# Cross-attention and expert FFN on one core: the transpose of the probabilities taken from TensorE to VectorE and DMA

## The chip, the core and the metric

The kernel runs on one core of a Trainium2 chip. A core has TensorE (matrix products into PSUM), VectorE, ScalarE and GpSimd (elementwise work), SyncE (which here issues most DMAs) and 16 DMA engines that move data between the chip's main memory (HBM) and the on-chip SBUF, or inside SBUF. PSUM has eight banks. Each engine runs its own instructions in order; engines wait for each other through semaphores. The metric is the device time of one execution in microseconds; a run's time is the median of several executions.

## The reference, cut to what matters

All data is f32. 32 batch elements (b), each with 128 tokens and 128 context rows, width 256; 16 heads of 64.

```python
lat = layer_norm(_layernorm(x)); ctx = layer_norm(ctx_1024)
q = lat @ Wq                                     # 128 x 1024 for each b
k, v = split(concatenate([ctx, lat]) @ Wkv)      # 256 keys for each b
dots = einsum('bhid,bhjd->bhij', q, k) * 64 ** -0.5
attn = softmax(dots, axis=-1)                    # 128 x 256 for each b and head
x = x + (einsum('bhij,bhjd->bhid', attn, v) -> 128 x 1024) @ Wout
# FFN on z = _layernorm(x): each token goes to the one of 8 experts with the largest z @ centroids.T
x = x + [z + sigmoid(affinity) * (relu(layer_norm_e(z) @ w1_e.T + b1_e) @ w2_e.T + b2_e)]
```

Product attn @ v sums over keys. TensorE sums over the partition axis of both operands, while softmax leaves queries on the partitions, so the probabilities have to be transposed: 128 x 256 values for each of 16 heads and 32 batch elements.

## The kernel before, in words

**Attention.** Batch elements go in 16 pairs (g). A pair takes four steps (r = 0 to 3), each with four heads for both elements of the pair: 64 steps u = 4g + r. Most operands are split into a high and a low part and multiplied in three passes (`PASSES`), the high part being written by ScalarE and the low part by VectorE. The V product and all transposes are plain f32 products.

In step u TensorE runs, in this order: `scores(u)` (12 pairs of small products into PSUM banks 0 to 3, one bank for each n = 2 * element + parity of the head); the transposes of the last step's probabilities n = 2 and 3, with the keys of step u+1 (`keys`, L508) between and behind them; in steps with r = 0 or 1 the transposes of the next pair's normalised inputs (`normed_t`, L487); a value product (`values`, L536); `transposes(u, 0)`; the queries of step u+1 (L522); `transposes(u, 1)`; the second value product; work of the last pair's rows (`ranks`, `wout`, `z_transposes`, `affinities`: a w_out product of 24 in steps r = 0 and 1); and last `outputs(u)`, the V product (L585), for element 0 of step u and element 1 of step u-1.

Around it: VectorE takes the row maxima of a bank of scores (`maxima`, L1048), ScalarE takes the exponentials and their sums (`exponentials`, L823), VectorE inverts the sums (L1054), GpSimd multiplies (`soften`, L1408), TensorE transposes (L564), VectorE copies the result from PSUM (`copy_transposed`, L1059), TensorE multiplies by V, ScalarE and VectorE split the result (`high_outputs` L832, `low_outputs` L1092). The probabilities have a single buffer: the exponentials of step u write where those of step u-1 stood.

**What sets the order.** Everything is written out by hand, for each engine, in `for u in range(n_steps)`. The results of TensorE other than scores go through PSUM banks 4 to 7 in turn. `bank_order` lists all these items in TensorE's order; item j has bank 4 + j % 4 and may begin once item j - 4 has been read.

**FFN.** Tokens' rows are written to a table in HBM, sorted by expert, with indirect DMAs (`scatter`); blocks of 256 rows (slots, 19 here) are read back and multiplied by their expert's w1 (`layer_1`, three passes) and w2 (`layer_2`, plain f32). The first slots run between and behind the last attention steps. SyncE loads each slot's weights (1 MB for w1, 1 MB for w2), rows and vectors, and before that writes eight pieces of padding of 792 KB (`filler`) behind the sorted rows.

## Time and profile before

| | |
|---|---|
| median of 3 timed runs | 1252.53 us (1252.13 to 1253.19) |
| the profiled execution | 1252.2 us, its span 1250.4 us |
| mean granted TensorE clock | 0.993 of full speed |
| busy: TensorE, VectorE, ScalarE, GpSimd | 1202.6, 830.0, 681.9, 531.6 us |
| DMA | 77.26 MB, 62 GB/s over the span |

A busy time adds up the time in which at least one instruction of the engine was in flight. TensorE's instructions overlap one another, so the time that a group of them really takes is read from its start and the start of the next group. In a group's row "idle before" is the engine's idle time ahead of it, and the engine named behind the arrow is what ended it. Lines (L564) are those of the kernel before.

### The profile page before, as it was taken

How to read it: one execution, taken by the hardware profiler on the slowest of the kernel's cores; microseconds unless marked ns; L12 is line 12 of the kernel's file. 1: busy time of each engine (PE TensorE's matmuls, PEld its weight loads, DVE VectorE, ACT ScalarE, POOL GpSimd, SP SyncE). 2: the span in 40 equal slices, each digit the busy share in tenths (PEclk: the TensorE clock that was granted, in tenths of full speed). 3: DMA queues.
4: the chain of work that ended last, by engine and by line, in shares of the span. 5: the costliest groups of instructions: out<-in, count | busy, mean ns of one | idle time of the engine just before them, and what ended most of it. 6: DMA issues, size and time to landing. Idle time of an engine off the chain costs nothing.

```text
span 1250.4 us, 26458 instructions
## 1 busy us (share of the span) xinstructions
PE 1202.6 (96%) x9730; PEld 1071.2 (86%) x9730; DVE 830.0 (66%) x2030; ACT 681.9 (55%) x1853; POOL 531.6 (43%) x716
## 2 busy tenths in 40 slices
PE   4899999999999999999999999999998899999995
PEld 4788888888888888888888888888887799999995
DVE  5566767677777777776868676777777665444441
ACT  4565646555656565555646464555555454545541
POOL 0454545454454444444445444545433452333321
PEclk9899999999999999999999999999999999999998
DMA  5000000000000000000000000000046435656560
GB/s 186 18 9 2 23 5 23 9 24 10 18 10 18 10 19 10 18 17 11 23 6 22 6 22 6 27 2 10 1 161 198 153 122 197 234 182 237 185 214 25
DMA packets 38116, 77.26 MB, mean 62 GB/s; under 512 B 6493, under 2 KB 30045, under 8 KB 33120
## 3 DMA queue, kind: packets, MB, share of 16 engines
q1 hardware_dynamic: 33808, 65.93, 15.8%
q0 software_dynamic: 3360, 8.53, 1.8%
q8 instruction: 82, 1.34, 0.4%
q10 hardware_dynamic: 816, 1.05, 0.3%
q14 instruction: 50, 0.41, 0.1%
HBM read 60.48 MB, written 15.79 MB: 61 GB/s over the span
## 4 chain that ended last, share of the span: by engine, by line
PE 89%; DVE 4%; ACT 3%; issue 1%; POOL 1%; DMA 0%; ACTq 0%; SPq 0%; POOLq 0%; DVEq 0%
PE psum L508 13%; PE psum L536 12%; PE psum L669 11%; PE psum L585 9%; PE psum L564 9%; PE psum L654 8%; PE psum L552 8%; PE psum L522 7%; PE psum L597 7%; ACT prob L823 1%; PE psum L487 1%; PE psum L605 1%; PE psum L612 1%; DVE neg_max L1048 1%; PE psum L633 1%
## 5 line engine op out<-in xcount | busy, mean ns | idle before, releaser
L1408 POOL TENSOR_TENSOR prob<-prob,inv_sum 128x512 f32<-128x512 f32 x256 | 266.0, 1040 | 370.8 <-DVE inv_sum L1054 369.3
L823 ACT ACTIVATE prob<-psum,neg_max 128x256 f32<-128x256 f32 x512 | 237.0, 472 | 95.6 <-DVE neg_max L1048 95.6
L1059 DVE COPY prob_t<-psum 128x512 f32<-128x512 f32 x256 | 174.5, 682 | 33.2 <-PE psum L564 33.0
L1048 DVE TENSOR_REDUCE neg_max<-psum 128x2 f32<-128x512 f32 x256 | 163.7, 681 | 0.0
L564 PE MATMUL psum<-ident,prob 128*128 128x128 f32 x1024 | 156.8, 276 | 1.7 <-ACT v_n L904 1.0
L564 PEld LDWEIGHTS psum<-ident,prob 128*128 128x128 f32 x1024 | 119.5, 140 | 28.2 <-ACT v_n L904 1.5
L832 ACT ACTIVATE head_out_hi<-psum 128x512 fp32r<-128x512 f32 (+1 forms) x65 | 38.4, 590 | 184.6 <-PE psum L585 182.8
L669 PE MATMUL psum<-w,v_n 128*128 128x256 f32 x608 | 134.4, 379 | 0.0
L585 PE MATMUL psum<-prob_t,v_n 128*64 128x128 f32 x2048 | 126.1, 276 | 1.1 <-DVE prob_t L1059 1.1
L669 PEld LDWEIGHTS psum<-w,v_n 128*128 128x128 f32 x608 | 114.2, 190 | 14.7
L585 PEld LDWEIGHTS psum<-prob_t,v_n 128*64 128x64 f32 x2048 | 110.7, 137 | 9.8 <-issue 5.3
L1477 POOL DMA_INDIRECT out<-x_in,r_ring x38 | 49.4, 1301 | 155.4 <-DVE x_in L1275 149.6
L804 ACT ACTIVATE k_hi<-psum 128x512 fp32r<-128x512 f32 x128 | 76.6, 598 | 54.0 <-PE psum L508 54.0
L1076 DVE TENSOR_TENSOR k_lo<-psum,k_hi 128x512 fp32r<-128x512 f32 x128 | 88.0, 687 | 25.1 <-ACT k_hi L804 24.7
L823 ACT ACTIVATION_READ_ACCUMULATOR prob<-psum,neg_max 128x1 f32 x512 | 104.5, 204 | 0.0
L815 ACT ACTIVATE v_n<-psum 128x512 f32<-128x512 f32 x128 | 76.5, 598 | 50.7 <-PE psum L536 50.7
L508 PE MATMUL psum<-kv_t_hi,w_hi 128*128 128x512 f32 x256 | 91.6, 439 | 4.8 <-DVE kv_t_lo L1070 2.7
L536 PE MATMUL psum<-w_hi,kv_t_hi 128*128 128x512 f32 x256 | 88.6, 427 | 0.0
L508 PE MATMUL psum<-kv_t_lo,w_hi 128*128 128x512 f32 x256 | 80.9, 398 | 0.0
L552 PE MATMUL psum<-k_hi,q_hi 64*128 64x256 f32 x512 | 79.1, 305 | 1.5 <-DVE q_lo L1083 1.5
L536 PE MATMUL psum<-w_lo,kv_t_hi 128*128 128x512 f32 x256 | 80.6, 396 | 0.0
L536 PE MATMUL psum<-w_hi,kv_t_lo 128*128 128x512 f32 x256 | 80.2, 395 | 0.0
(149 smaller groups left out, 2589.4 us busy)
## 6 DMA issues: line engine op xcount, KB each, us to landing
w_ring<-in_experts SPq DMA_DIRECT2D x19, 1024.0 KB, 5.5
w<-in_experts SPq DMA_DIRECT2D x19, 1024.0 KB, 7.5
sorted_rows<-filler SPq DMA_DIRECT2D x8, 792.0 KB, 7.5
r_ring<-sorted_rows SPq DMA_DIRECT2D x19, 264.0 KB, 2.7
x_in<-in_x SPq DMA_DIRECT2D x16, 256.0 KB, 2.7
c_in<-in_ctx_in SPq DMA_DIRECT2D x16, 256.0 KB, 3.0
x_in<-in_b SPq DMA_DIRECT2D x19, 128.0 KB, 6.9
w_ring<-in_w_out SPq DMA_DIRECT2D x1, 1024.0 KB, 5.5
```

Source lines behind the costliest of these rows:

```text
L508: last = pe.matmul(bank.rearrange("p (b t) -> p b t", b=2), k_w[hw][:, c, col:col + P], kv_t[hx][:, c, slot:slot + 2, :], start=(n == 0 an ...
L536: last = pe.matmul(bank, kv_t[hx][:, c, slot, side * P:(side + 1) * P], v_w[hw][:, c, col:col + BANK], start=(n == 0 and c == 0), stop=(n ...
L552: ins = pe.matmul(psum[:, 2 * bb + parity, i * 2 * P:(i + 1) * 2 * P], q_s[hq][rows, u % 2, i, bb * P:(bb + 1) * P], k_s[hk][rows, u % 2, ...
L564: last = pe.transpose(bank[:, (2 * i + side) * P:(2 * i + side + 1) * P], prob[:, n, i, side * P:(side + 1) * P], ident[:])
L585: last = pe.matmul(bank[rows, (2 * bb + i) * P:(2 * bb + i + 1) * P], v_n[:, h % 2, bb, side, head * DH:(head + 1) * DH], prob_t[:, 2 * bb ...
L654: last = pe.matmul(dst, w1_hl[hw][s % NW][:, c, f * P:(f + 1) * P], xn_hl[hx][:, s % 2, c, :], start=(n == 0 and c == 0), stop=(n == 2 and ...
L669: last = pe.matmul(bank[:, i * d_model:(i + 1) * d_model], hid[:, s % 2, f, i * P:(i + 1) * P], w2[:, f * d_model:(f + 1) * d_model], star ...
L823: act.activation(prob[:, n, i, :], psum[:, n, i * 2 * P:(i + 1) * 2 * P], ACT.Exp, bias=neg_max[:, at, i:i + 1], accum_out=prob_sum[:, at, ...
L1048: dve.tensor_reduce(neg_max[:, (4 * u + n) % 8, :], psum[:, n, :].rearrange("p (i j) -> p i j", i=2), AXIS_X, ALU.max, negate=True).then_i ...
L1059: last_reads(item, dve.tensor_copy(prob_t[:, n].rearrange("p i s t -> p (i s t)"), work_bank(number[item])))
L1076: last_reads(item, dve.tensor_tensor(k_s[1][:, u % 2, i, :], work_bank(number[item]), k_s[0][:, u % 2, i, :], ALU.subtract))
L1408: pool.tensor_tensor(probs, probs, inv_sum[:, (4 * u + n) % 8, :, None].to_broadcast([P, 2, 2 * P]), ALU.mult).then_inc(s_soft, 1)
```

## The change

The transposes leave TensorE. VectorE transposes the probabilities in place, in blocks of 32 x 32, after GpSimd's multiplication, and DMAs move the blocks to the partitions where they belong. For this the probabilities are stored in another order: key j of a side stands at block j % 4, row j // 4, so that ScalarE reads the scores from PSUM with a step of four elements. Four DMAs (one for each quarter of the partitions) of 32 x 4 pieces of 1 KB move one batch element of a step; the target has two buffers, one of them in the ring of the w1 weights (`w_ring` in the rows).

```diff
-                    item = ("t", u, n)
-                    wait_made(dve, item)
-                    last_reads(item, dve.tensor_copy(prob_t[:, n].rearrange("p i s t -> p (i s t)"), work_bank(number[item])))
+                def transpose_blocks(u, n):
+
+                    dve.wait_ge(s_soft, 4 * u + n + 1)
+                    blocks = prob[:, n // 2, :, n % 2].rearrange("p j i s k -> p j (i s k)")
+                    dve.transpose(blocks, blocks).then_inc(s_quad, 1)
...
+                def move_probabilities(u, bb):
+
+
+                    sp.wait_ge(s_quad, 4 * u + 2 * bb + 2)
+                    if u >= 2:
+                        wait_made(sp, ("pv", u - 2))
+                    for a in range(4):
+                        sp.dma_start(prob_t[u % 2][:, bb, a].rearrange("p h i s q -> p (h i s q)"),
+                                     prob[a * Q:(a + 1) * Q, bb].rearrange("p j h i s q -> p j (h i s q)")
+                                     ).then_inc(s_prob_t[bb], 16)
+
+                for u in range(n_steps + 1):
...
 
                 def exponentials(u, n):
+
                     act.wait_ge(s_max, 4 * u + n + 1)
-                    if n >= 2 and u >= 1:
-                        wait_made(act, ("t", u - 1, n))
+                    bb, parity = divmod(n, 2)
+                    if u >= 1:
+                        act.wait_ge(s_prob_t[bb], 4 * 16 * u)
                     at = (4 * u + n) % 8
                     for i in range(2):
-                        act.activation(prob[:, n, i, :], psum[:, n, i * 2 * P:(i + 1) * 2 * P], ACT.Exp,
-                                       bias=neg_max[:, at, i:i + 1],
+                        scores_i = psum[:, n, i * 2 * P:(i + 1) * 2 * P].rearrange("p (s k j) -> p j s k", s=2, j=4)
+                        act.activation(prob[:, bb, :, parity, i], scores_i, ACT.Exp, bias=neg_max[:, at, i:i + 1],
                                        accum_out=prob_sum[:, at, i:i + 1]).then_inc(s_exp, 1)
 
                 def high_outputs(u):
...
                 def soften(u, n):
                     pool.wait_ge(s_inv, 4 * u + n + 1)
-                    probs = prob[:, n]
-                    pool.tensor_tensor(probs, probs, inv_sum[:, (4 * u + n) % 8, :, None].to_broadcast([P, 2, 2 * P]),
-                                       ALU.mult).then_inc(s_soft, 1)
+                    probs = prob[:, n // 2, :, n % 2].rearrange("p j i s k -> p j i (s k)")
+                    inverse = inv_sum[:, (4 * u + n) % 8, None, :, None].to_broadcast([P, 4, 2, 2 * Q])
+                    pool.tensor_tensor(probs, probs, inverse, ALU.mult).then_inc(s_soft, 1)
 
                 chained = [0]
```

ScalarE's exponentials of step u now wait for the moves of step u-1. The V product of step u is taken whole, for both elements, at the end of step u+1 (for the last step, in the tail), and what depends on it is a step later too: the w_out products stand in steps r = 1 and 2.

```diff
-                def transposes(u, n):
-                    bank = begin(("t", u, n))
-                    pe.wait_ge(s_soft, 4 * u + n + 1)
-                    for i in range(2):
-                        for side in range(2):
-                            last = pe.transpose(bank[:, (2 * i + side) * P:(2 * i + side + 1) * P],
-                                                prob[:, n, i, side * P:(side + 1) * P], ident[:])
-                    last.then_inc(s_job, 1)
-
                 def outputs(u):
                     bank = begin(("pv", u))
-                    for bb, at in ((0, u), (1, u - 1)):
-                        if not 0 <= at < n_steps:
...
                         weights_split(K_REST)
-                    if u > 0:
-                        transposes(u - 1, 2)
                     if following:
                         keys(u + 1, 0)
-                    if u > 0:
-                        transposes(u - 1, 3)
-                    if following:
                         keys(u + 1, 1)
                     for pair, side in inputs_of(u, n_pairs):
                         normed_t(pair, side)
-                    h = values_made(u)
-                    if u == 0:
+                    now = values_made(u, n_pairs)
+                    if u == 1:
                         weights_split(V_REST)
-                    if h < 2 * n_pairs:
-                        values(h, r % 2, 0)
-                    if not following:
-                        layer_1(0)
-                    transposes(u, 0)
+                    for item in now[:1]:
+                        values(*item[1:])
                     if u == 0:
                         weights_split(Q_REST)
                     if following:
                         queries(u + 1)
-                    transposes(u, 1)
-                    if h < 2 * n_pairs:
-                        values(h, r % 2, 1)
-                    if u == 4:
+                    for item in now[1:]:
+                        values(*item[1:])
+                    if not following:
+                        layer_1_plain()
+                    if u == 5:
                         pe.wait_ge(s_const, 4 * 16)
                         pe.wait_ge(s_wo_split, 2)
...
                         z_transposes(2 * g - 2)
                         wout(2 * g - 1)
-                    if r == 2 and g >= 1:
+                    if r == 3 and g >= 1:
                         affinities(2 * g - 2)
                         z_transposes(2 * g - 1)
-                    if r == 3 and g >= 1:
-                        ranks(2 * g - 2)
-                        affinities(2 * g - 1)
                     if u == n_steps - 2:
                         row_transposes(0)
-                    outputs(u)
-                transposes(n_steps - 1, 2)
-                transposes(n_steps - 1, 3)
+                    if u > 0:
```

On SyncE the moves stand in one queue with all other loads, in the order of the steps:

```diff
+                    g, r = divmod(u, 4)
+                    if u > 0:
+                        move_probabilities(u - 1, 1)
+                    if r == 0 and g + 2 < n_pairs:
+                        load_pair(g + 2)
+                    if u == n_steps - 4:
+                        sp.wait_ge(s_table, 1)
+                        scattered(early_batches)
+                        sp.wait_ge(s_wlo, len(pieces))
+                        sp.wait_ge(s_wo_split, 2)
+                        for s in range(2):
+                            load_rows(s)
+                            load_vectors(s)
+                        load_weights_1(0)
+                    if u == n_steps - 2:
+                        fill_tails()
+                    if u == n_steps - 1:
+                        wait_made(sp, ("q", n_steps - 1))
+                        load_weights_2(0)
+                        load_b2(0)
+                        load_weights_1(1)
+                    if u < n_steps:
+                        move_probabilities(u, 0)
                 for s in range(2, n_early):
```

The first layer of slot 0 becomes a plain f32 product without split operands. The tail (what comes behind the 64 steps) has another order on all engines; TensorE's is

```diff
+                def layer_1_plain():
+
+                    for i in range(FC // 2):
+                        bank = begin(("h", i))
+                        if i == 0:
+                            wait_read(pe, ("ft", 0))
+                            pe.wait_ge(f_w1[0], 16)
+                        for f in (2 * i, 2 * i + 1):
+                            for c in range(KC):
+                                last = pe.matmul(bank[:, (f % 2) * BLOCK:(f % 2 + 1) * BLOCK],
+                                                 w1_ring[:, 0, c * d_ff + f * P:c * d_ff + (f + 1) * P], xn[:, c, :],
+                                                 start=(c == 0), stop=(c == KC - 1))
+                        last.then_inc(s_job, 1)
...
-                    outputs(u)
-                transposes(n_steps - 1, 2)
-                transposes(n_steps - 1, 3)
+                    if u > 0:
+                        outputs(u - 1)
+                ranks(n_batches - 4)
+                affinities(n_batches - 3)
                 row_transposes(1)
+                layer_2(0)
+                ranks(n_batches - 3)
+                outputs(n_steps - 1)
+                layer_1(1)
                 wout(n_batches - 2)
-                outputs(n_steps)
-                ranks(n_batches - 3)
-                layer_2(0)
                 row_transposes(2)
                 wout(n_batches - 1)
                 z_transposes(n_batches - 2)
-                layer_1(1)
+                layer_1(2)
                 affinities(n_batches - 2)
-                layer_1(2)
-                ranks(n_batches - 2)
-                z_transposes(n_batches - 1)
                 row_transposes(3)
                 layer_2(1)
+                z_transposes(n_batches - 1)
+                ranks(n_batches - 2)
+                layer_1(3)
                 affinities(n_batches - 1)
-                layer_1(3)
+                row_transposes(4)
+                layer_2(2)
                 ranks(n_batches - 1)
-                row_transposes(4)
                 totals(("total",), n_batches - 1)
-                layer_2(2)
```

**VectorE, at the turn from a step with r = 1 to the next.** Before: the split of the V product, the first maxima, then copies of transposed probabilities (`prob_t<-psum`).

```order
L1106 BN_AGGR mv_z<-stats_z 128x2
L1092 TENSOR_TENSOR head_out_lo<-psum,head_out_hi 128x2x256
L1048 TENSOR_REDUCE neg_max<-psum 128x2 x2
L1059 COPY prob_t<-psum 128x512
L1048 TENSOR_REDUCE neg_max<-psum 128x2 x2
L1054 RECIPROCAL inv_sum<-prob_sum 128x2
L1059 COPY prob_t<-psum 128x512
L1076 TENSOR_TENSOR k_lo<-psum,k_hi 128x512
```

The same place now:

```order
L1151 BN_AGGR mv_z<-stats_z 128x2
L1137 TENSOR_TENSOR head_out_lo<-psum,head_out_hi 128x2x256
L1106 STREAM_TRANSPOSE prob<-prob 128x4x128
L1094 TENSOR_REDUCE neg_max<-psum 128x2 x2
L1106 STREAM_TRANSPOSE prob<-prob 128x4x128
L1094 TENSOR_REDUCE neg_max<-psum 128x2 x2
L1100 RECIPROCAL inv_sum<-prob_sum 128x2
L1123 TENSOR_TENSOR k_lo<-psum,k_hi 128x512
L1100 RECIPROCAL inv_sum<-prob_sum 128x2
L1123 TENSOR_TENSOR k_lo<-psum,k_hi 128x512
L1106 STREAM_TRANSPOSE prob<-prob 128x4x128
L1100 RECIPROCAL inv_sum<-prob_sum 128x2
```

A transpose of the last step's third quarter (n = 2) stands ahead of the first maxima, that of its fourth (n = 3) behind them, and the first of this step (n = 0) behind the keys.

**SyncE, steps 62 and 63.** Before, the fills and the first w2 load follow each other without anything between:

```order
L448 DMA sorted_rows<-filler 128x6x264
...
L404 DMA w_0<-in_experts 128x2048
...
L420 DMA x_in<-in_b 128x256
...
L412 DMA vec_ring<-in_experts 128x12
...
L425 DMA r_ring<-sorted_rows 128x2x264
```

Now (the last of the eight fills, and what follows; the loads of registers in between are left out):

```order
L463 DMA sorted_rows<-filler 128x6x264
L473 DMA prob_t<-prob 128x1x256 x8
...
L423 DMA w_0<-in_experts 128x2048
...
L439 DMA x_in<-in_b 128x256
...
L416 DMA w_kv<-in_experts 128x2048
L473 DMA w_ring<-prob 128x1x256 x8
```

The move of step 62's first element and that of its second (eight DMAs together) stand behind all eight fills; the moves of step 63 stand behind slot 0's w2, b2 and slot 1's w1.

## Rows read from the trace of the kernel before

**Rows 1.** The page: busy time by engine, and the chain's shares.
```profile
PE 1202.6 (96%) x9730; PEld 1071.2 (86%) x9730; DVE 830.0 (66%) x2030; ACT 681.9 (55%) x1853; POOL 531.6 (43%) x716
...
PE 89%; DVE 4%; ACT 3%; issue 1%; POOL 1%; DMA 0%; ACTq 0%; SPq 0%; POOLq 0%; DVEq 0%
```

**Rows 2.** Timeline of TensorE: start, us, engine, line, operation, shapes, records.
```profile
606.50 0.39 PE L552 MATMUL psum<-k_hi,q_hi 64*128 64x256 f32 x2
...
608.54 0.71 PE L508 MATMUL psum<-kv_t_hi,w_hi 128*128 128x512 f32 x2
...
610.01 0.60 PE L564 MATMUL psum<-ident,prob 128*128 128x128 f32 x4
...
611.84 0.63 PE L536 MATMUL psum<-w_hi,kv_t_hi 128*128 128x512 f32 x2
...
613.23 0.60 PE L564 MATMUL psum<-ident,prob 128*128 128x128 f32 x4
613.58 0.48 PE L522 MATMUL psum<-kv_t_hi,w_hi 128*128 128x256 f32 x2
...
619.70 0.39 PE L552 MATMUL psum<-k_hi,q_hi 64*128 64x256 f32 x2
...
631.14 1.20 PE L597 MATMUL psum<-w_o_hi,head_out_hi 128*128 128x256 f32 x8
...
634.19 1.97 PE L585 MATMUL psum<-prob_t,v_n 128*64 128x128 f32 x32
636.09 0.39 PE L552 MATMUL psum<-k_hi,q_hi 64*128 64x256 f32 x2
```

**Rows 3.** Timeline of ScalarE in the same step.
```profile
606.62 0.60 ACT L832 ACTIVATE head_out_hi<-psum 128x512 fp32r<-128x512 f32 x1 [2.01 <-PE psum L585]
...
613.92 0.47 ACT L823 ACTIVATE prob<-psum,neg_max 128x256 f32<-128x256 f32 x1
```

**Rows 4.** Timeline of VectorE in the same step.
```profile
608.11 1.28 DVE L1048 TENSOR_REDUCE neg_max<-psum 128x2 f32<-128x512 f32 x2
609.30 0.68 DVE L1059 COPY prob_t<-psum 128x512 f32<-128x512 f32 x1
...
614.96 0.17 DVE L1054 RECIPROCAL inv_sum<-prob_sum 128x2 f32<-128x2 f32 x1 [0.41 <-ACT prob L823]
615.92 0.69 DVE L1083 SCALAR_TENSOR_TENSOR q_lo<-psum,q_hi 128x512 fp32r<-128x512 f32 x1 [0.79 <-ACT q_hi L809]
```

**Rows 5.** Groups by line: two VectorE passes inside SBUF; busy us, mean ns.
```profile
L1251 DVE CAST k_hi<-c_in 128x512 fp32r<-128x512 f32 x19 | 8.7, 457 | 23.0 <-ACT c_in L887 23.0
...
L1164 DVE TENSOR_TENSOR w_lo<-r_ring,w_hi 128x1024 fp32r<-128x1024 f32 x2 | 2.4, 1222 | 0.3 <-ACT w_hi L854 0.3
```

**Rows 6.** DMA issues: queue, count, KB each, median us from issue to landing.
```profile
x_in<-in_x SPq DMA_DIRECT2D x16, 256.0 KB, 2.7
...
x_in<-in_b SPq DMA_DIRECT2D x19, 128.0 KB, 6.9
...
vec_ring<-in_experts SPq DMA_DIRECT2D x19, 6.0 KB, 1.6
```

**Rows 7.** Timeline of SyncE's DMA issues, at the start and at the fills.
```profile
19.34 0.37 SPq L388 DMA_DIRECT2D w_ring<-in_w_out  x1
19.75 0.58 SPq L369 DMA_DIRECT2D x_in<-in_x  x1
...
930.60 13.50 SPq L448 DMA_DIRECT2D sorted_rows<-filler  x8
```

**Rows 8.** Busy time in windows: engines, granted clock, DMA share, GB/s.
```profile
940.00:950.00 10.00, 9.66 (x96) 8.67 (x96) 4.23 (x12) 4.63 (x14) 4.42 (x10) 1.00 1.07 341
```

**Rows 9.** Timeline of TensorE: a first layer's start after a wait; a later slot.
```profile
967.84 0.47 PE L654 MATMUL psum<-k_hi,w_hi 128*128 128x256 f32 x2 [2.08 <-DVE k_lo L1253]
...
1100.01 0.59 PE L654 MATMUL psum<-k_hi,w_hi 128*128 128x256 f32 x2
...
1106.38 7.07 PE L669 MATMUL psum<-w,v_n 128*128 128x256 f32 x32
```

More of the change, by code:

```diff
@@ L17 @@
 BANK = 512
+Q = 32
 OUT_OF_RANGE = 1 << 20
@@ L329, in wait_made, with heads_at, heads_out @@
                     eng.wait_ge(s_job, made_before[item] + 1)
-            def heads_out(buffer, u):
-                r = u % 4
-                first, end = (0 if u < n_steps else 1), (2 if u > 0 else 1)
-                return buffer[:, first:end, 2 * r:2 * r + 2, :], slice(first * 2 * P, end * 2 * P)
+            def heads_at(b, c):
+                return (b // 2 * HC + c) % (HC + 2)
+            def heads_out(h, u):
+                at = heads_at(u // 4 * 2, 2 * (u % 4))
+                return head_out[h][:, :, at:at + 2, :] if at < HC else heads_over[h][:]
             def wait_first_layer(eng, s):
@@ L943, in _ @@
                         gain_bias(pair, side)
-                    if h < 2 * n_pairs:
-                        read_values(h, r % 2, 0)
+                    for item in now[:1]:
+                        read_values(*item[1:])
                     exponentials(u, 2)
```

307 lines of the change are left out of this document (155 added, 152 removed).

## Prediction

> **What bounds the kernel now.** I read the page's busy shares first: TensorE is busy 96% of the span, VectorE 66%, ScalarE 55%, GpSimd 43%; the chain that ended last is TensorE for 89% of its length [rows 1]. The reader is to see that one engine sets the time and none of the others is near its limit, but this says nothing about what one TensorE instruction is worth. For that I read TensorE's timeline by the starts of its groups, because durations of pipelined matmuls overlap. A light step of the attention (one without a product with w_out) runs from the first score product at 606.50 to the next at 619.70, 13.20 us; the step behind it, with that product, takes 16.39 us, until 636.09 [rows 2]. Two light and two heavy steps make a group of 59.2 us, and there are 16 groups. No idle time stands in these rows, so what leaves TensorE is won, until something else closes a round of waits inside a step. Then I read ScalarE's and VectorE's timelines in the same step for the pieces of such a round [rows 3, 4], and last the queue of the transfers, which the change loads most [rows 6 to 8].
>
> **What leaves TensorE.** Each step loses four groups of four transposes. One stands from 613.23 to 613.58, 0.35 us, so 1.40 us for the four. The product right behind such a group is dearer than one that follows another product: the key product after a group takes 608.54 to 610.01, 1.47 us, the value product after a key product 611.84 to 613.23, 1.39 us [rows 2]. Four such transitions go, 4 x 0.085 = 0.34 us. Together 1.74 us a step, 64 steps: **-111 us**. (The sum of busy times on the page would have promised more, since the records overlap.) TensorE alone would then need 13.20 - 1.74 = 11.46 us for a step with r = 3. The w_out products move from r = 0, 1 to r = 1, 2. The step with r = 0 gives up 3.05 us of them (631.14 to 634.19) and gets an affinity, by the V products' pace (32 records in 1.90 us, 634.19 to 636.09) about 0.24 us: 16.39 - 1.74 - 3.05 + 0.24 = 11.84 us [rows 2]. The heavy ones need 14.6 us.
>
> **What VectorE gets.** It loses 256 copies of 128x512 out of PSUM, which follow each other at 0.60 us (608.11 to 609.30 is two maxima of the same size, the copy behind them lasts 0.68) [rows 4], and gets 256 transposes of the same size inside SBUF. No row shows such an instruction. A cast of 128x512 between SBUF tiles took 457 ns, which is the lower end; the upper is a pass of twice the elements, 128x1024 in 1222 ns [rows 5]. I take 0.60 us, the row of the same size that it replaces; VectorE's total then does not change. The Trainium skill (VectorE: DVE Perf Modes, "The three transpose paths") gives 311 ns for a 128x128 bf16 tile on VectorE and says that it only turns 32x32 blocks; by that figure as a stand-in for 128 elements a partition, four times the elements less the start-up would be near 0.7 us, and the sum would be the same within a few us. No run here shows it.
>
> **What the transfers cost.** Each half step (a batch element) now issues four DMAs of 128 KB on SyncE's queue, 512 in all. They are not on a chain by their volume: 1 MB a step of 12 us is 87 GB/s, while the queue has moved 341 GB/s in one stretch [rows 8]. What counts is the time L from the last transpose to ScalarE's release, because the probabilities are single-buffered: the exponentials of step u+1 write where step u's moves read. A 6 KB load lands 1.6 us after issue, one of 256 KB in rows of 1 KB 2.7 us [rows 6]: 262 KB in 1.1 us is 238 GB/s. 524 KB at this rate take 2.2 us, so 1.6 + 2.2, and I add 0.3 for two semaphore hops: L = 4.1 us. The issues (19.34 to 19.75, 0.41 us apart [rows 7]) fit under that. Lower end: issue-bound, 3 x 0.41 + 1.6 + 0.4 + 0.3 = 3.5 us. Upper end: the slowest 128 KB row, the b2 load, lands after 6.9 us behind a megabyte [rows 6]; three issues more make 8.1 us.
>
> **The round inside a step.** Let S be the start of step u's scores. Behind V of the step before, head_out_hi starts at S + 0.12 and lasts 0.60 [rows 3], head_out_lo then ends at S + 1.4. VectorE next runs transpose (u-1,2), 0.6; two maxima, 1.2; transpose (u-1,3), 0.6: S + 3.8. The moves land at S + 3.8 + L. Only then may the exponentials (u,2) start; from 613.92 to the reciprocal at 614.96 they take 1.04 [rows 3, 4], the reciprocal and the transpose (u,1) behind it 0.75, q_lo 0.6 (0.69 long at 615.92 [rows 4]). V's product takes the PSUM bank that q_lo frees (the fourth item before it in the bank order) and needs 1.90. With two hops of 0.05: step = 8.2 + L = 12.3 us. That is over both light steps, by 12.3 - 11.46 = 0.84 and 12.3 - 11.84 = 0.46 us, 16 times each: **+21 us**. Heavy steps have 2.3 us of cover. The other half's round (transpose (u,1) at S + 9.6, landed at S + 13.7, exponential (u+1,0) wanted at 12.3 + 2.7 = 15.0) has 1.3 us to spare. The strided read of the scores by ScalarE and the reordered GpSimd product are not priced by any row; each is hidden until it adds 1 us, except 2 x the extra of an exponential in the round, for which I take nothing and keep 0.4 us (+13) in the range.
>
> **The end.** At u = 60 five loads stand ahead of the move (60,0) on SyncE's queue; at 1.69 us an issue, as for the eight fills (13.50 us [rows 7]), the queue is free at S + 13.8 and the megabyte among them drains first; the move lands near S + 18 instead of the 15 wanted: **+3 us**. At u = 62 the eight fills (6.49 MB) are issued between move (61,1) and move (62,0). At 341 GB/s [rows 8] they drain in 19 us from S + 5.4, so the move lands near S + 26.5, and exponential (63,0), wanted at 14.6 + 2.7 = 17.3, is 9 us late: **+9 us**. Slot 0's first layer in plain f32 has 32 records instead of 48; the same number takes 7.07 us in a second layer, against 6.37 less 0.43 for the transposes in between, 5.94 us, from 1100.01 to 1106.38: **+1 us** [rows 9]. In return its split of w1 and of its input disappears, and with it such waits as the 2.08 us before 967.84 [rows 9] and the queueing on VectorE around it; I credit **-5 us** to the new tail, with 8 either way.
>
> **Sum** against the profiled execution's 1252.2 us (span 1250.4; the median of the timed runs, 1252.53, is 0.3 higher, which is less than these terms can resolve): 1252.2 - 111 + 21 + 3 + 9 + 1 - 5 = **1170 us**.
>
> **Rivals.**
> *The moves are free.* L is 3.5 us and the fills hide: light steps wait 0.24 us in one of four, 4 us in all; 1252.2 - 111 + 4 + 3 + 1 - 5 = 1144. For it: 1 KB rows moved at 341 GB/s [rows 8]. Against it: nothing on the queue ran in four small pieces.
> *Half the ports.* Each DMA reads 32 partitions. If that halves the 341 GB/s to 170, 524 KB need 3.1 us, L = 5.0, the light steps take 13.2, (1.74 + 1.36) x 16 = 50 instead of 21: 1199. For it: the 128 KB load that reads one row again and again is the slowest in rows 6; against it, its wait is mostly the queue ahead of it. The Trainium skill (SBUF — State Buffer, "Door 1: The DMA port swizzle") says that partitions 0 to 31 reach 8 of the 16 DMA ports and gives 189 GB/s for them at 1 MiB; by that figure L would be about 4.7 us, an estimate, and the time near 1190. This is the rule that speaks against the change; the trace of before has no transfer out of SBUF's quarter to test it.
> *Dear transposes.* At 1.2 us each, the three in the round add 1.8 us: light steps 14.1, 4.9 x 16 = 78: 1227.
> *Slower than before.* The round trip of the probabilities becomes the step's bound in every step. The place is SyncE's queue between transpose (u-1,3) and exponential (u,2); all four steps then take 8.2 + L. With some 8 us for the end this decides from L = 6.5 us on (4 x 14.7 = 58.7), a rate under 116 GB/s. At the upper end, L = 8.1, a group takes 65.2 us: 1252.2 + 96 + 8 = 1356. For it: the 6.9 us row; against: four times 256 KB in 2.7.
>
> **Chances.** Forecast 0.49 (1155 to 1186), free moves 0.17, half ports 0.15, dear transposes 0.08 (0.02 of it no change), slower 0.11. The range runs from below the free moves (1140) over the half ports with 0.4 us more in the round (1220) and leaves out the last two cases. What this kernel's measurement can tell from no change is 0.2%, 2.5 us. Faster 0.87, same 0.02, slower 0.11.
>
> **What the profile after would show.** TensorE's identity transposes of prob gone, and 1.4 us between key product and next key product; light steps of 12.3 us with idle time of about 0.5 to 0.9 us before the V product (or before the next scores), put down to q_lo; heavy steps near 14.6 without any; ScalarE's exponentials (u,2) waiting for a DMA in light and heavy steps alike; transposes at 0.7 us; the moves' landing about 2.2 to 2.5 us after each issue; one gap of some 9 us around step 63. I am wrong if exponential (u,0) waits for its move in ordinary steps, if light and heavy steps are equally long (the round binds all), or if VectorE is busy above 90% in a light step (transposes dearer than 1 us).

## The result: slower, and the profile after

The changed kernel takes **1304.69 us** (median of 4 runs, 1299.49 to 1307.05) against 1252.8 us for the kernel before on the same chip: **1.0409 times as long [1.0374, 1.0444]**. The forecast was 1170 us, at most 1220, with 0.11 for slower. Sign and size were both wrong.

The profiled execution took 1306.52 us. Its page, busy time by engine and the chain's shares:

```profile
span 1304.6 us, 24812 instructions
PE 1146.6 (88%) x8690; PEld 1017.5 (78%) x8690; DVE 835.8 (64%) x2026; ACT 663.1 (51%) x1851; POOL 527.4 (40%) x716
...
PE 58%; DVE 16%; ACT 11%; DMA 6%; SPq 5%; issue 3%; POOL 0%; ACTq 0%; DVEq 0%; POOLq 0%
```

Against [rows 1] TensorE has 1040 instructions fewer (9730 to 8690), nearly all of them the transposes, yet is busy only 56 us less. Its share fell from 96% to 88%, and the chain, 89% TensorE before, now runs through VectorE, ScalarE and the transfers as well. So TensorE waits for others inside the steps, and the busy time that is left got dearer: the mean granted clock is 0.941, it was 0.993.

Where it closed is read from the starts of the score products. The mean length of a step by its place r in the group of four, over the 14 inner groups of each trace, in us:

| | r=0 | r=1 | r=2 | r=3 | group | first score to score 63 | score 63 to the end |
|---|---|---|---|---|---|---|---|
| before | 16.38 | 16.54 | 13.17 | 13.22 | 59.3 | 938.7 | 287.4 |
| forecast | 12.3 | 14.6 | 14.6 | 12.3 | 53.8 | | |
| after | 13.14 | 14.86 | **18.30** | **15.28** | 61.6 | 972.7 | 307.9 |

Steps r=0 and r=1 are near the forecast; r=2 and r=3, the two that also transpose the final rows z, are 3.7 and 3.0 us over it. TensorE's longest waits (engine, operand and line, waited for; us in total, times, longest):

```profile
PE psum L643 <- ACT z_buf L885: 76.6, 30, 3.2
PE psum L621 <- DVE q_lo L1130: 15.9, 14, 1.4
PE psum L650 <- ACT v_n L949: 8.6, 1, 8.6
```

The wait that I forecast, the V product's for q_lo, is there with 15.9 us. One that I did not forecast is five times as large: the transposes of z (L643) wait for ScalarE's z_buf, 30 times. Before, that wait was 6.5 us over 16 times. TensorE's timeline in a step with r=2 and the one behind it:

```profile
609.64 0.62 PE L584 MATMUL psum<-w_hi,kv_t_lo 128*128 128x512 f32 x2
613.00 0.41 PE L643 MATMUL psum<-ident,z_buf 128*128 128x128 f32 x2 [2.74 <-ACT z_buf L885]
613.17 0.72 PE L635 MATMUL psum<-w_o_hi,head_out_hi 128*128 128x256 f32 x4
...
617.71 1.97 PE L621 MATMUL psum<-w_ring,v_n 128*64 128x128 f32 x32
619.61 0.39 PE L600 MATMUL psum<-k_hi,q_hi 64*128 64x256 f32 x2
...
628.27 0.51 PE L650 MATMUL psum<-cent,z_t 128*128 128x8 f32 x4
631.20 0.66 PE L643 MATMUL psum<-ident,z_buf 128*128 128x128 f32 x2 [2.42 <-ACT z_buf L885]
631.79 3.25 PE L621 MATMUL psum<-prob_t,v_n 128*64 128x128 f32 x32
634.97 0.39 PE L600 MATMUL psum<-k_hi,q_hi 64*128 64x256 f32 x2
```

ScalarE in the first of these steps, with what SyncE issued ahead of it:

```profile
607.48 0.60 ACT L858 ACTIVATE v_n<-psum 128x512 f32<-128x512 f32 x1 [0.46 <-PE psum L584]
609.95 0.47 ACT L869 ACTIVATE prob<-psum,neg_max 128x256 f32<-128x256 f32 x1 [1.87 <-DMA w_ring<-prob]
...
610.86 0.59 ACT L852 ACTIVATE q_hi<-psum 128x512 fp32r<-128x512 f32 x1
611.34 0.48 ACT L869 ACTIVATE prob<-psum,neg_max 128x256 f32<-128x256 f32 x1
...
612.24 0.62 ACT L885 ACTIVATE z_buf<-row_ring 128x256 f32<-128x256 f32 x1
```

```profile
605.32 2.49 SPq L473 DMA_DIRECT2D w_ring<-prob  x4
```

Exponential (u,2) waits for the move of the step before until 609.95. Behind it in ScalarE's order stand q_hi, exponential (u,3) and only then z_buf, 612.24 to 612.86. TensorE wanted z_buf at about 610.3 (613.00 less the 2.74 us that it waited). Of all that ScalarE had to do, z_buf needed nothing from the move; it only stood behind something that did.

The idle time is not all. The product with w_out behind it took 613.17 to 617.71, 4.54 us, where before it took 3.05 [rows 2]; the V product of the next step 3.18 us from 631.79, not 1.90. Windows over these stretches (length; busy us of PE, PEld, DVE, ACT, POOL; granted clock; DMA share; GB/s):

```profile
610.10:613.00 2.90, 0.16 (x1) 0.03 (x1) 1.91 (x6) 2.90 (x11) 1.39 (x2) 1.00 0.00 0
...
614.40:617.30 2.90, 2.90 (x15) 2.90 (x15) 0.10 (x1) 0.00 (x0) 1.21 (x4) 0.50 0.43 109
617.70:619.60 1.90, 1.90 (x33) 1.73 (x32) 1.03 (x3) 0.00 (x0) 0.51 (x2) 1.00 0.00 0
...
631.80:634.90 3.10, 3.10 (x33) 3.00 (x32) 1.78 (x8) 1.69 (x4) 0.95 (x4) 0.57 0.59 147
```

TensorE stood still for 2.74 us, began again, and from about a microsecond later was granted 0.50, which is its 1.2 GHz level, for some 3 us; in the second stretch the clock was low (0.57 on average) as soon as it began again. It is so nearly everywhere: of the 24 idle stretches of 2.4 to 3.2 us between 60 and 850 us of this trace, 23 have such a low stretch behind them. Nearly every such wait is paid for a second time.

### The profile page after: what moved, and what is told of

It is laid out like the page before. It is cut to its first block, busy times and chain, and to the rows that moved or that the text cites. A ratio compares the mean times of both kernels' runs of the same rounds, so it can differ in the third digit from the quotient of the medians.

```text
span 1304.6 us, 24812 instructions
## 1 busy us (share of the span) xinstructions
PE 1146.6 (88%) x8690; PEld 1017.5 (78%) x8690; DVE 835.8 (64%) x2026; ACT 663.1 (51%) x1851; POOL 527.4 (40%) x716
## 4 chain that ended last, share of the span: by engine, by line
PE 58%; DVE 16%; ACT 11%; DMA 6%; SPq 5%; issue 3%; POOL 0%; ACTq 0%; DVEq 0%; POOLq 0%
PE psum L718 10%; PE psum L635 9%; PE psum L621 8%; PE psum L703 8%; PE psum L584 7%; ACT prob L869 6%; PE psum L556 6%; DVE neg_max L1094 4%; DMA w_ring<-prob 4%; PE psum L570 4%; SPq L473 4%; DVE prob L1106 4%; PE psum L600 3%; ACT q_hi L852 2%; DMA prob_t<-prob 2%
## 5 line engine op out<-in xcount | busy, mean ns | idle before, releaser
L1106 DVE STREAM_TRANSPOSE prob<-prob 128x512 f32<-128x512 f32 x256 | 178.3, 697 | 1.1 <-POOL prob L1453 1.1
L1094 DVE TENSOR_REDUCE neg_max<-psum 128x2 f32<-128x512 f32 x256 | 160.0, 663 | 0.0
L718 PE MATMUL psum<-w,v_n 128*128 128x256 f32 x608 | 138.8, 388 | 0.0
L1100 DVE RECIPROCAL inv_sum<-prob_sum 128x2 f32<-128x2 f32 x256 | 40.2, 157 | 148.6 <-ACT prob L869 145.4
L876 ACT ACTIVATE head_out_hi<-psum 128x512 fp32r<-128x512 f32 x52 | 31.2, 600 | 151.6 <-PE psum L621 151.5
L584 PE MATMUL psum<-w_hi,kv_t_hi 128*128 128x512 f32 x256 | 83.6, 408 | 8.8 <-DVE k_lo L1123 8.8
L556 PE MATMUL psum<-kv_t_hi,w_hi 128*128 128x512 f32 x256 | 87.2, 422 | 2.7 <-DVE kv_t_lo L1117 2.7
L643 PE MATMUL psum<-ident,z_buf 128*128 128x128 f32 x64 | 16.5, 349 | 76.6 <-ACT z_buf L885 76.6
L621 PE MATMUL psum<-prob_t,v_n 128*64 128x128 f32 x1024 | 82.1, 328 | 0.0
L556 PE MATMUL psum<-kv_t_hi,w_lo 128*128 128x512 f32 x256 | 79.6, 392 | 0.0
```

The source lines that it names most:

```text
L556: last = pe.matmul(bank.rearrange("p (b t) -> p b t", b=2), k_w[hw][:, c, col:col + P], kv_t[hx][:, c, slot:slot + 2, :], start=(n == 0 an ...
L584: last = pe.matmul(bank, kv_t[hx][:, c, slot, side * P:(side + 1) * P], v_w[hw][:, c, col:col + BANK], start=(n == 0 and c == 0), stop=(n ...
L621: last = pe.matmul(bank[rows, (2 * bb + i) * P:(2 * bb + i + 1) * P].rearrange("p (a q) -> p a q", a=4), v_n[:, h % 2, bb, side, head * DH ...
L718: last = pe.matmul(bank[:, i * d_model:(i + 1) * d_model], hid[:, s % 2, f, i * P:(i + 1) * P], w2[:, f * d_model:(f + 1) * d_model], star ...
L1094: dve.tensor_reduce(neg_max[:, (4 * u + n) % 8, :], psum[:, n, :].rearrange("p (i j) -> p i j", i=2), AXIS_X, ALU.max, negate=True).then_i ...
L1106: dve.transpose(blocks, blocks).then_inc(s_quad, 1)
```

## The experiments

Theory A: z_buf's place behind the exponentials that wait for the move makes the idle time, the clock doubles part of it, and a round of 8.2 + L with single-buffered probabilities is the smaller rest. Rival B: something else that the change does sets the steps (transfers that disturb TensorE or its weight loads, the depth of the banks, dearer instructions), and the wait for z_buf only names whoever comes last.

Every run was compared with the kernel before on its own chip (1251.98 to 1252.42 us). Step lengths are as in the table above:

| | us (median, range) | ratio to before [95%] | r=0 | r=1 | r=2 | r=3 |
|---|---|---|---|---|---|---|
| z_buf early | 1217.07 (1214.29 to 1221.8) | 0.9722 [0.9693, 0.975] | 13.62 | 14.91 | 13.70 | 13.35 |
| 10 idle products | 1277.27 (1273.01 to 1282.75) | 1.021 [1.0173, 1.0246] | 13.20 | 14.87 | 17.43 | 14.00 |
| 24 idle products | 1262.85 (1259.8 to 1266.87) | 1.0088 [1.0061, 1.0116] | 13.28 | 14.88 | 16.62 | 13.90 |
| two buffers | 1179.78 (1178.94 to 1180.59) | 0.9421 [0.9405, 0.9436] | 11.86 | 14.40 | 14.69 | 12.00 |
| both | 1161.29 (1160.16 to 1165.98) | 0.9281 [0.9257, 0.9305] | 11.86 | 14.43 | 13.70 | 11.48 |
| early, two DMAs a move | 1192.35 (1191.75 to 1192.86) | 0.9517 [0.9501, 0.9534] | 12.24 | 14.75 | 13.70 | 11.61 |
| early, half the bytes | 1193.50 (1187.63 to 1194.35) | 0.9513 [0.9483, 0.9542] | 12.79 | 14.81 | 13.70 | 12.37 |
| both, fills split | 1161.21 (1159.11 to 1163.1) | 0.9273 [0.9251, 0.9295] | 11.86 | 14.43 | 13.70 | 11.48 |
| both, fills earlier | 1158.24 (1156.69 to 1158.54) | 0.9246 [0.9231, 0.9261] | 11.85 | 14.40 | 13.70 | 11.48 |

### z_buf ahead of the exponentials that wait

```diff
                         read_values(*item[1:])
+                    if r == 2 and g >= 1:
+                        norm_x1(2 * g - 2)
+                    if r == 3 and g >= 1:
+                        norm_x1(2 * g - 1)
                     exponentials(u, 2)
...
-                    if r == 2 and g >= 1:
-                        norm_x1(2 * g - 2)
-                    if r == 3 and g >= 1:
-                        norm_x1(2 * g - 1)
```

> Changed kernel with one move on ScalarE: the activation that writes z_buf (norm_x1) stands ahead of the exponentials (u, 2) in steps r = 2 and 3 instead of behind (u, 3). Theory A (queue): the transposes of z wait 2.4 to 2.7 us because z_buf stands behind exponentials that wait for a DMA; then both gaps and the half-clock stretches behind them go, r = 3 falls from 15.3 to about 13.1 us (the round of the moves, as in r = 0), r = 2 from 18.3 to 14.3 to 15, and the time from 1304 to about 1215 us. Theory B (round): the round of the moves bounds r = 2 and 3 by itself through the bank of the queries; the wait only changes its name, time above 1290 us.

Measured: 1217.07 us, 88 us less than the changed kernel, by one instruction's place in ScalarE's order. The wait for z_buf is gone (0.2 us in all), step r=2 is 13.70. TensorE's waits up to 900 us now:

```profile
PE psum L621 <- DVE q_lo L1130: 41.1, 28, 1.9
PE psum L635 <- DVE q_lo L1130: 3.0, 2, 1.6
```

What follows: A's first part is shown, and the second largest wait has stepped forward, the round that I had worked out. It shows in both light steps now, and a long one can again cost clock: TensorE's timeline of a step with r=3 in this kernel, which took 14.08 us against 12.9 to 13.0 for most of its kind.

```profile
620.85 1.97 PE L621 MATMUL psum<-w_ring,v_n 128*64 128x128 f32 x32
622.75 0.39 PE L600 MATMUL psum<-k_hi,q_hi 64*128 64x256 f32 x2
...
633.99 2.92 PE L621 MATMUL psum<-prob_t,v_n 128*64 128x128 f32 x32 [1.80 <-DVE q_lo L1130]
636.83 0.58 PE L600 MATMUL psum<-k_hi,q_hi 64*128 64x256 f32 x2
```

### Products of no use in the idle time

Two kernels let TensorE transpose the identity while it waits for z_buf; all that stands in the wait's way stays as it is in the changed kernel. The second has 24 in place of 10.

```diff
                     bank = begin(("zt", b))
+                    if b < n_batches - 2:
+                        for i in range(10):
+                            pe.transpose(bank[:, 2 * P:3 * P], ident[:], ident[:])
                     pe.wait_ge(s_z, b + 1)
```

> Changed kernel with ten extra transposes of the identity by TensorE in the bank that the transposes of z will use, ahead of their wait for z_buf (steps r = 2 and 3); they fill the idle time with work whose result nobody reads. Theory A (idle time costs twice, by the gap and by the clock behind it): the granted clock in the w_out product behind (0.64) returns to 1, r = 2 falls from 18.3 to about 16.8 us, r = 3 from 15.3 to about 14.0, time about 1260 us. Theory B (the clock falls with the total load, or costs nothing because other engines set the pace there): no change or slower, 1304 or more.

Measured: 1277.27 us, not 1260. Step r=3 fell to 14.0 in most groups, but r=2 was either 16.6 or near 18.6. Ten products last 1.25 us and leave holes, in TensorE's timeline:

```profile
593.29 1.25 PE L643 MATMUL psum<-ident 128*128 128x128 f32 x10
596.73 0.44 PE L646 MATMUL psum<-ident,z_buf 128*128 128x128 f32 x2 [2.19 <-ACT z_buf L888]
601.45 1.97 PE L621 MATMUL psum<-w_ring,v_n 128*64 128x128 f32 x32
...
612.37 1.29 PE L643 MATMUL psum<-ident 128*128 128x128 f32 x10
614.83 0.44 PE L646 MATMUL psum<-ident,z_buf 128*128 128x128 f32 x2 [1.17 <-ACT z_buf L888]
615.20 1.97 PE L621 MATMUL psum<-prob_t,v_n 128*64 128x128 f32 x32
```

Behind the hole of 2.19 us, z transposes and w_out product took 4.72 us (596.73 to 601.45), as slow as in the changed kernel (613.00 to 617.71, 4.71); the V product behind the hole of 1.17 lasted its full-speed 1.97. The dose was too small to decide, so it was raised.

> The changed kernel with 24 extra transposes of the identity ahead of the wait for z_buf instead of 10 (nobody reads them). Ten lasted 1.25 us and left 2.2 us of idle time in many steps r = 2, where the clock still fell. 24 last about 2.8 us and cover the wait. Theory A (half of a gap's price is the clock behind it): the same wait, but every step r = 2 at 16.6 and r = 3 at 13.8 us instead of 18.3 and 15.3; time 1304 - 16 x 3.2 = about 1256 us. Theory B (the clock follows something other than TensorE's idle time): no further gain over 1277 us, or slower.

Measured: 1262.85 us. Every inner step with r=2 now takes 16.5 to 17.0 and nearly every one with r=3 13.9. In the whole trace 2.0 us of waiting for z_buf are left, in 3 waits, and the mean granted clock is 0.980, where the changed kernel's was 0.941. TensorE's timeline:

```profile
590.41 0.44 PE L646 MATMUL psum<-ident,z_buf 128*128 128x128 f32 x2
593.61 1.97 PE L621 MATMUL psum<-w_ring,v_n 128*64 128x128 f32 x32
...
604.53 2.81 PE L643 MATMUL psum<-ident 128*128 128x128 f32 x24
607.49 1.97 PE L621 MATMUL psum<-prob_t,v_n 128*64 128x128 f32 x32
620.69 1.97 PE L621 MATMUL psum<-w_ring,v_n 128*64 128x128 f32 x32 [1.21 <-DVE q_lo L1133]
```

The z transposes and the w_out product take 3.20 us (590.41 to 593.61), not 4.71, at full clock:

```profile
590.00:597.00 7.00, 6.98 (x86) 6.44 (x84) 3.68 (x13) 1.44 (x3) 3.89 (x11) 1.00 0.33 78
```

What follows: nothing in z_buf's way was changed, and the kernel is still 42 us faster. That is what the lower clock cost: 18.30 - 16.62 = 1.68 and 15.28 - 13.90 = 1.38 us in a group, times 14 inner groups 43 us. Theory A had said about 1256 us; some low clock is left (a step r=0 of 14.12 us, for one). The rest of what the early z_buf gained is the waiting itself, 76.6 us in the changed kernel, less what the round takes back there: with z_buf early the waits for q_lo grew from 15.9 to 41.1 us.

### A second buffer for the probabilities

Odd steps write their probabilities into w1_ring's first half, which is free until the expert weights come, so an exponential waits for the move of the step before the last. The order on ScalarE is that of the changed kernel.

```diff
+            prob_odd = w1_ring[:, 0].rearrange("p (b j h i s k) -> p b j h i s k", b=2, j=4, h=2, i=2, s=2)
+            def odd(u):
+                return u % 2 == 1 and 3 <= u <= n_steps - 7
+            def prob_of(u):
+                return prob_odd if odd(u) else prob[:]
...
-                        act.wait_ge(s_prob_t[bb], 4 * 16 * u)
+                        last = max([w for w in range(u) if odd(w) == odd(u)], default=-1)
+                        if last >= 0:
+                            act.wait_ge(s_prob_t[bb][last % 2], 4 * 16 * (last // 2 + 1))
...
-                        act.activation(prob[:, bb, :, parity, i], scores_i, ACT.Exp, bias=neg_max[:, at, i:i + 1],
+                        act.activation(prob_of(u)[:, bb, :, parity, i], scores_i, ACT.Exp, bias=neg_max[:, at, i:i + 1],
```

> Changed kernel with two buffers for the probabilities in steps 3 to 57 (the second in the first w1 ring slot), so that exponentials wait for the moves of the step before the last only. Theory A (the single buffer closes the round 8.2 + L, L = 4.9): all steps come down to TensorE's work, 11.5 to 12 us for r = 0 and 3, 14.2 to 14.8 for r = 1 and 2, group 52 to 53 us instead of 61.6, time about 1165 us. Theory B (ScalarE or VectorE are late by their own load and order): z_buf still late, group above 58 us, time above 1245 us.

> Both edits together: z_buf early on ScalarE and two buffers for the probabilities. Theory A: no more than 10 us under the second buffer alone, since with it the exponentials are early anyway: about 1160 us. Theory B (two independent causes): the two gains add, well under 1120 us.

Measured: 1179.78 us with the buffer alone, 15 more than expected, and 1161.29 with the early z_buf too, a further gain of 18 us where at most 10 were expected. With both, TensorE between 100 and 700 us reads, under the same columns as the windows above, after it the changed kernel's row:

```profile
100.00:700.00 600.00, 599.50 (x5198) 530.22 (x5198) 498.70 (x1321) 374.87 (x1162) 323.68 (x482) 1.00 0.41 98
```

```profile
100.00:700.00 600.00, 535.95 (x4335) 470.34 (x4334) 427.48 (x1103) 321.60 (x977) 271.94 (x403) 0.95 0.34 81
```

What follows: with both waits gone TensorE is all but never idle, at full clock, with the same moves running (98 GB/s with all other transfers). That rules B out for the ordinary steps: neither the transfers nor VectorE (83% busy here) holds TensorE up. The light steps are 11.86 and 11.48 us, where the forecast's term for TensorE alone said 11.84 and 11.46: the -111 us are real. The two repairs overlap: 88 alone, 125 alone, 143 together, since either takes most of the other's wait away. With the buffer alone 22.3 us of waiting for z_buf are left, for ScalarE has its other work ahead of it, and r=2 stays 1.0 us longer.

### What L is made of

Two kernels with z_buf early move less. In the first, steps from u = 2 on issue two DMAs of 128 KB a move in place of four; in the second, four of 64 KB, in pieces of 512 bytes. Both leave half of the probabilities unmoved, so that the V products read old ones.

```diff
-                    for a in range(4):
+                    for a in range(4 if u < 2 else 2):
```

```diff
-                        sp.dma_start(prob_t[u % 2][:, bb, a].rearrange("p h i s q -> p (h i s q)"),
-                                     prob[a * Q:(a + 1) * Q, bb].rearrange("p j h i s q -> p j (h i s q)")
+                        hs = 2 if u < 2 else 1
+                        sp.dma_start(prob_t[u % 2][:, bb, a, 0:hs].rearrange("p h i s q -> p (h i s q)"),
+                                     prob[a * Q:(a + 1) * Q, bb, :, 0:hs].rearrange("p j h i s q -> p j (h i s q)")
```

> The kernel with z_buf early, and from step 2 on only two of the four DMAs of each move (half of the probabilities are not moved; the output uses stale ones). Base for the comparison is z early alone: 1217 us, steps r = 0 and 3 of 13.0 us when undisturbed, L about 4.8. Theory A (L = three issues of 0.62 us before the last, 2.7 us for its landing, 0.3 for hops): two issues fewer take 1.24 us off L, light steps stop at 11.8 us (r = 0) and 11.5 to 11.8 (r = 3), time 1217 - 32 x 1.2 = about 1179 us, less by a few us more if the clock's dips go. Theory B (bytes from 32 partitions set L): L falls by half of the 2.2 us of transfer, 1.1, and the time is nearly the same; the half-bytes kernel tells them apart.

> The kernel with z_buf early, and from step 2 on all four DMAs of each move but with half the bytes (pieces of 512 B instead of 1 KB; the other half is not moved and stale). Theory A (issue-bound): L loses only what the last DMA's own transfer shortens, 0.1 to 0.3 us; light steps 12.8 to 13.0, time 1208 to 1217 us. Theory B (bytes from 32 partitions set L): L falls by 1.1 us as with two moves, time about 1182 us.

Measured: 1192.35 and 1193.5 us. The medians must not be compared with each other: with old probabilities the tokens of the first go to other experts, it loads 21 slots instead of 19, its TensorE has 8858 instructions, the second 8690, and it takes 331.5 us from score 63 on, the second 311.8. The steps can. Issues in the page's list (DMAs, KB each, us to landing), of the first and of the second:

```profile
prob_t<-prob SPq DMA_DIRECT2D x132, 128.0 KB, 2.7
w_ring<-prob SPq DMA_DIRECT2D x132, 128.0 KB, 2.7
```

```profile
prob_t<-prob SPq DMA_DIRECT2D x248, 64.0 KB, 2.2
w_ring<-prob SPq DMA_DIRECT2D x248, 64.0 KB, 2.1
```

What follows: L can be read directly, from the end of transpose (u-1,3) to the start of exponential (u,2). In steps with r=3 its median is 4.7 us with z_buf early, 4.15 with half the bytes and 3.4 with half the issues as well; the steps take 12.9 to 13.0 (where no clock is lost), 12.37 and 11.61 us. So 256 KB less are worth 0.55 us, and two issues less 0.75 us on top: two intervals, some 1.3 us, less the 0.5 us that a DMA of 128 KB takes longer to land than one of 64 KB. Steps with r=0 lie higher, with medians of 13.45, 12.81 and 12.26 us, since that transpose ends 4.26 us into them and not 3.85. The three intervals between issues, 1.9 us, are thus a larger part of L than what half the bytes save, but neither theory had the whole: up to score 63 half the bytes gained 27 us, between the 0 to 9 of A and the 35 of B, and half the issues with them 49 us, more than the 38 of A.

### The fills at the end

On top of both repairs, the eight fills were taken from their place ahead of move (62,0) and put in fours behind moves (62,0) and (63,0), and in a second kernel behind (61,0) and (62,0).

```diff
-                    if u == n_steps - 2:
-                        fill_tails()
...
                         move_probabilities(u, 0)
+                    if u in (n_steps - 2, n_steps - 1):
+                        fill_tails(range((u - n_steps + 2) * 4, (u - n_steps + 3) * 4))
```

> The kernel with z_buf early and two buffers (1161 us), and the eight fills split: four behind move (62, 0), four behind move (63, 0), instead of eight ahead of move (62, 0). Theory A (the fills hold the move back, exponential (63, 0) waits 16.7 us for it and TensorE 13.7 us ahead of an affinity behind the plain first layer): the wait ahead of the affinity falls to 2 to 5 us, time 1149 to 1153 us. Theory B (the wait belongs to the plain first layer and its reading, which come too early in the order): it stays above 10 us and the time above 1157 us.

> z_buf early and two buffers (1161 us), with four fills behind move (61, 0) and four behind move (62, 0), so that the fills do not stand ahead of step 63's moves or among the first weights. Theory A (the tail waits for the transfers crowded into steps 62 and 63: 0.96 of the DMA engines' time there): the wait of 13.7 us ahead of the affinity falls below 5 us and nothing takes its place: 1148 to 1153 us. Theory B (the tail's order of work sets it, as the split into steps 62 and 63 suggested, which moved the wait and won nothing): 1157 us or more.

Measured: 1161.21 us, no change, and 1158.24 us, 3 us less; both expectations were missed. TensorE's wait ahead of the last affinity did fall, from 13.7 us to 7.0 and 6.0. In the first kernel other engines took it over; waits from 850 to 960 us:

```profile
ACT y_t L930 <- DMA r_ring<-sorted_rows: 13.3, 2, 11.1
POOL sorted_rows L1512 <- DMA sorted_rows<-filler: 13.2, 1, 13.2
```

GpSimd's scatter may not start before the filler lies in its place, and what reads the sorted rows comes behind the scatter. In the second kernel step 62 grew to 19.2 us instead (14.1 without the edit). The fills cost something in each of these places; where the rest of the end's time goes, these two runs do not say. The version with the fills earlier is the fastest measured: 0.9246 [0.9231, 0.9261] of the kernel before.

## Why the prediction was wrong

**The step that failed** is the sentence "Heavy steps have 2.3 us of cover", and with it the claim that the round binds only as 8.2 + L through q_lo and the V product. I followed one consumer of ScalarE's delayed work and read off from it which steps had time to spare. I did not list what else stood behind the exponentials that now wait. z_buf stood there, in the steps r=2 and r=3, and its consumer sits on TensorE right behind the last value product, in a heavy step 5 us before the V product's end (629.99 to 635.07 in the kernel with both repairs). There was no cover for it at all: 2.74 us of waiting in r=2, 2.42 in r=3, and the clock's share on top.

**The sum had no term for the clock.** Nothing in the trace of before had priced a wait inside a step, and I took a wait at its length. A wait of this size costs 1.4 to 1.7 us more, some 43 us of the whole, by the kernel with 24 idle products.

Point by point, for the profiled executions (1306.5 against 1170):

- *TensorE, -111 us*: right. 11.86 and 11.48 us in the kernel with both repairs, forecast 11.84 and 11.46. The heavy steps came out below the forecast's 14.6, at 14.43 (r=1) and 13.70 (r=2).
- *VectorE's transposes, 0.60 us each*: right. The next instruction starts 0.61 to 0.63 us behind one, and it lasts 0.70 (page of after, below). The Trainium skill's route (VectorE: DVE Perf Modes, "The three transpose paths") gave near 0.7, and this row agrees with it. "Dear transposes" was wrong.

```profile
L1106 DVE STREAM_TRANSPOSE prob<-prob 128x512 f32<-128x512 f32 x256 | 178.3, 697 | 1.1 <-POOL prob L1453 1.1
```

- *L = 4.1 us*: 4.7 us, from the transpose's end near 605.3 to 609.95. I had made it of 1.6 us and 2.2 us for 524 KB at one rate, with the issues fitting under that. They do not: four issues fill 2.49 us, 0.62 us apart (I had 0.41 from [rows 7]), and the last DMA needs its whole 2.7 us to land: 605.32 + 1.87 + 2.7 = 609.9. That also answers "the moves are free", which wanted 3.5. The formula itself held where its starting point does: 8.2 + 4.7 = 12.9, and 12.9 to 13.0 is what undisturbed steps with r=3 take with z_buf early; those with r=0 take 13.0 to 13.7. By the formula the term is 1.4 + 1.1 = 2.5 us in a group, +40 us for 16, instead of +21.
- *Half the ports, L = 5.0*: the number came near; whether its reason holds stays open. The intervals between issues are 1.9 of the 4.7 us, and no rival had them at this size. But a 128 KB move out of 32 partitions lands 2.7 us after its issue, as long as 256 KB across all partitions took before (3.2 us for `x_in` in the changed kernel), and a 64 KB one 2.1 to 2.2: about 0.55 us for 64 KB, some 120 GB/s for one move, an estimate, and half of the 238 GB/s that I had worked out from [rows 6]. No run reads the same bytes out of all partitions, which would decide it. The Trainium skill (SBUF — State Buffer, "Door 1: The DMA port swizzle") led to about 4.7 us for L; that agrees in size, and the runs neither show nor rule out its reason.
- *The strided read of the scores, nothing*: right. 478 ns an exponential, 472 before.
- *The chance of a slower kernel*: I gave the right mechanism's name, a round trip that binds, to the wrong resource and to a threshold (L = 6.5 us in all steps) that never came into play.
- *Up to score 63*: forecast -87 us (-111 + 21 + 3), measured +34. Of the 121 us between, the two z steps hold 3.7 + 3.0 us in each of the 14 inner groups, 94, and the steps r=0 and r=1 0.84 + 0.26, 15; the remaining 12 lie in the first and the last group, where single steps take up to 22.9 us. With both repairs the same stretch is 825.9 us, 113 less than before.
- *The end*: forecast +9 + 1 - 5 = +5, measured 307.9 - 287.4 = +20.5. Exponential (63,0) waited 11.7 us for its move, which the eight fills delayed by 14.22 us on the queue, near the +9:

```profile
982.07 2.50 SPq L473 DMA_DIRECT2D w_ring<-prob  x4
985.40 14.22 SPq L463 DMA_DIRECT2D sorted_rows<-filler  x8
999.72 8.94 SPq L473 DMA_DIRECT2D prob_t<-prob  x8
```

```profile
998.30 7.17 PE L684 MATMUL psum<-c_in,w_ring 128*128 128x256 f32 x32
1014.08 1.02 PE L650 MATMUL psum<-cent,z_t 128*128 128x8 f32 x4 [8.60 <-ACT v_n L949]
```

  The credit of 5 us for the new tail is not to be seen. Windows from score 63 on, of after and of before:

```profile
997.00:1304.50 307.50, 276.68 (x1752) 256.48 (x1748) 139.91 (x251) 134.57 (x266) 90.77 (x86) 0.94 0.53 182
```

```profile
963.00:1250.00 287.00, 268.35 (x1772) 250.34 (x1770) 139.75 (x244) 132.88 (x266) 92.75 (x85) 0.98 0.49 170
```

  TensorE is idle for 30.8 us instead of 18.7 and busy 8.3 us longer, with fewer instructions, at 0.94 instead of 0.98. That the lower clock is all of the 8.3 us is my reading; no run separates it from the new tail's own work. All variants take 302 to 312 us there (but for the one whose tokens go to other experts), so this part stays open.
- *The signs that I named*: the exponentials (u,2) do wait for a DMA in nearly every step (66 waits, 138 us), the V product does wait for q_lo, exponential (u,0) waits for the row maxima and not for its move, and the moves land at 2.7, not 2.2 to 2.5. The sign that fell is "heavy steps near 14.6 us without any" idle time: it holds for r=1 (14.86) and fails for r=2, which is the failed step again.

## What to carry to other kernels

When a change makes an engine wait for something new, write down every instruction behind that wait in its order, and for each of them who takes it and when; cover worked out for one consumer says nothing of the next. An instruction that needs nothing of the new wait is moved ahead of it: here that was worth 88 us, against 52 us that the change had lost. Price a wait of more than 2 us on TensorE at its length plus the stretch at half clock behind it, and break a long round (a single buffer with a DMA in it) before trimming its parts: with z_buf early, the second buffer took 58 us off the time up to score 63, while half the bytes took off 27 and half the bytes in half the issues 49, and those two kernels move only half of the data.

## What the runs showed of the hardware

- Idle stretches of TensorE of 2.4 to 3.2 us were followed in 23 of 24 cases in the changed kernel by some 3 us at a granted clock of 0.50 (1.2 GHz): w_out product 4.54 us instead of 3.05, V product 3.18 instead of 1.90. Shorter ones gave no sharp limit: with z_buf early, 7 of 22 stretches of 1.4 to 1.9 us had it behind them (1.80 us before 633.99 did, 1.84 before 800.89 did not), and most of some 1.2 us did not. Products of no use in the gap kept the clock up, and paid for themselves (42 us).
- DMAs from one SBUF tile to another, of 128 KB in 1 KB pieces or 64 KB in 512-byte pieces, are issued 0.62 us apart on SyncE's queue; two loads at the start were 0.41 us apart [rows 7]. A move of 128 KB landed 2.7 us after its issue whether two or four stood together.
- 98 GB/s of transfers over 600 us, most of them such moves, took nothing off TensorE: 599.50 us busy of 600, clock 1.00, and light steps of 11.86 and 11.48 us where the forecast had made 11.84 and 11.46 from the rows of before.
